# Decoder layer on one core: low parts of q, k and the row maxima by a negative identity in PSUM and ScalarE copies, and three more halves by C on VectorE

## What is computed

```python
# mixer, state scan in chunks of 64 tokens, 512 channels x 16 states
delta = softplus(dlt @ W_dt.T + b_dt)
dA, dBu = exp(delta x A), delta * Bm * u
carry = dA * carry + dBu;  y = sum_n carry[.., n] * C[.., n]
x = layernorm(x + (y * silu(res)) @ W_out.T + b_out)
# cross-attention
q, k, v = x @ w_q.T + b_q, ctx @ w_k.T + b_k, ctx @ w_v.T + b_v
x = layernorm(x + softmax(q k^T / sqrt(16)) v @ w_o.T + b_o)
# experts
x = layernorm(x + (silu(x @ w1) * (x @ w3)) @ w2)
```

## Time and profile before

| | |
|---|---|
| three runs | 2802.23, 2810.59, 2811.07 us, median 2810.59 |
| span of the profiled execution | 2799.9 us (the page gives no other time for it) |
| PE busy | 2426.5 us, 87% |
| DVE busy | 2139.4 us, 76% |
| ACT busy | 1804.7 us, 64% |
| POOL busy | 2075.6 us, 74% |
| granted TensorE clock, mean | 0.955 |

### The profile page before, as it was taken

The page is one execution under the profiler, slowest core; times in us unless marked ns, Lnnn a source line. Parts: engine busy times, 40 slices in busy tenths (PEclk is TensorE's granted clock), DMA queues, the critical chain, the costliest instruction groups (busy, mean ns, idle before and its releaser), DMA issues. The chain is left out here.

```text
span 2799.9 us, 49777 instructions
## 1 busy us (share of the span) xinstructions
PE 2426.5 (87%) x14816; PEld 1658.8 (59%) x14816; DVE 2139.4 (76%) x3586; ACT 1804.7 (64%) x3972; POOL 2075.6 (74%) x968
## 2 busy tenths in 40 slices
PE   3678888888888888988888889988887869999998
PEld 2355666666666666666666666666665545555554
DVE  1778999999999999999999999999999622322332
ACT  1666878878888888788777878778887531211111
POOL 2999999999999999999999999999999300000000
PEclk8788999999999999999999999999998869999999
DMA  3455676656666666666666666665666350243221
GB/s 117 128 133 149 154 168 166 157 157 157 165 167 161 157 167 174 160 171 170 163 166 162 164 165 171 169 169 159 157 166 158 92 159 12 86 128 98 78 78 31
DMA packets 319323, 399.65 MB, mean 143 GB/s; under 512 B 115697, under 2 KB 256241, under 8 KB 314962
## 3 DMA queue, kind: packets, MB, share of 16 engines
q1 hardware_dynamic: 303698, 384.91, 52.9%
q10 hardware_dynamic: 15360, 11.55, 1.5%
HBM read 300.86 MB, written 94.37 MB: 141 GB/s over the span
## 5 line engine op out<-in xcount | busy, mean ns | idle before, releaser
L496 POOL TENSOR_TENSOR arena<-arena 128x1024 f32<-128x1024 f32 x512 | 1209.3, 2366 | 59.6 <-DMA arena<-w_dram 35.4
L572 ACT ACTIVATE dA_ps<-arena,a_neg 128x252 f32<-128x252 f32 x2048 | 868.9, 461 | 327.7 <-DVE dA_ps L777 171.8
L754 DVE TENSOR_TENSOR_SCAN arena<-dA_ps,arena 128x512 f32<-128x512 f32 x672 | 803.4, 1208 | 110.6 <-ACT dA_ps L572 92.2
L506 POOL TENSOR_TENSOR arena<-arena 128x1024 f32<-128x1024 f32 (+1 forms) x416 | 809.1, 1945 | 16.3 <-DVE arena L754 15.3
L754 DVE TENSOR_TENSOR_SCAN dA_ps<-dA_ps,arena 128x512 f32<-128x512 f32 x352 | 416.3, 1206 | 4.8 <-POOL arena L496 3.7
L819 DVE TENSOR_REDUCE mx<-s_ps 128x2 f32<-128x512 f32 x512 | 344.3, 672 | 35.5 <-PE s_ps L877 35.5
L877 PE MATMUL a_ps<-xT,w_conv 128*128 128x256 f32 x1536 | 368.0, 389 | 0.0
L630 ACT ACTIVATE probs<-st_ps 128x512 f32<-128x512 f32 x512 | 296.6, 579 | 42.0 <-PE st_ps L877 34.9
L877 PEld LDWEIGHTS a_ps<-xT,w_conv 128*128 128x128 f32 x1536 | 287.2, 193 | 53.7 <-issue 16.5
L877 PE MATMUL s_ps<-k_st,q_st 96*128 96x256 f32 x1024 | 269.6, 346 | 48.6 <-DVE mx L819 35.1
L877 PE MATMUL y_ps<-arena,sel 128*32 128x256 f32 x4096 | 259.4, 395 | 52.7 <-DVE m_rows L825 28.5
(11 more groups left out here) (105 smaller groups left out, 3213.4 us busy)
## 6 DMA issues: line engine op xcount, KB each, us to landing
arena<-delta_dram SPq DMA_DIRECT2D x512, 128.0 KB, 2.9
arena<-w_dram SPq DMA_DIRECT2D x512, 128.0 KB, 3.3
arena<-bc_dram SPq DMA_DIRECT2D x128, 256.0 KB, 4.5
q_st<-q_parts_dram SPq DMA_DIRECT2D x512, 64.0 KB
k_st<-k_parts_dram SPq DMA_DIRECT2D x512, 64.0 KB
w_dram<-u SPq DMA_DIRECT2D x32, 512.0 KB, 3.1
delta_dram<-delta SPq DMA_DIRECT2D x32, 512.0 KB, 3.9
k_parts_dram<-parts SPq DMA_DIRECT2D x32, 512.0 KB, 3.9
```

The lines of the kernel that those rows point to most:

```text
L496: pool.tensor_tensor(dBu[:, n % NB], w_r[:, n // RP % 2, t % RP].unsqueeze(1).to_broadcast([P, QS, L]), bc_r[:, b.par, 0], ALU.mult).then_ ...
L506: pool.tensor_tensor(h[:, n % NH, states], h[:, n % NH, states], bc_r[:, b.par, 1, states], ALU.mult).then_inc(s_hC, 1)
L572: last = nc.scalar.activation(dA[n % NDA][:, q, :, 1:], delta_r[:, n // (2 * RP) % 2, t % RP].rearrange("p (c t) -> p c t", t=CH)[:, :, 1: ...
L754: nc.vector.tensor_tensor_scan(dst, decays, dBu[:, n % NB, 2 * half:2 * half + 2].rearrange("p q t -> p (q t)"), 0.0, ALU.mult, ALU.add).t ...
```

## The change

`low` for q and k and `max_low` become two steps each. TensorE adds a negative identity times the high part to the value that still stands in PSUM (`less_high`, one matmul of 128x512 into `a_ps`; `max_less_high`, one of 8x128 into `y_ps`), and ScalarE copies what is left (`low`, `max_low`, now in ScalarE's block). The maxima now keep their sign, and the constant rows of `k_st` are -1 in place of 1. `x1T_evac` moves from VectorE, slot 9, to ScalarE, slot 8. `HC_DVE` gets (3, 1), (12, 1) and (13, 1), so VectorE multiplies 14 halves, and GpSimd's product of tiles 3, 12 and 13 shrinks from 1024 to 512 columns.

```diff
-HC_DVE = [(1, 0), (1, 1), (4, 1), (5, 0), (5, 1), (6, 1), (8, 0), (9, 1), (10, 0), (10, 1), (14, 1)]
+HC_DVE = [(1, 0), (1, 1), (3, 1), (4, 1), (5, 0), (5, 1), (6, 1), (8, 0), (9, 1), (10, 0), (10, 1), (12, 1), (13, 1), (14, 1)]
...
-            nc.gpsimd.memset(k_st[4 * DK:4 * DK + 2].bitcast(F32), 1.0).then_inc(s_const_p, 1)
+            nc.gpsimd.memset(k_st[4 * DK:4 * DK + 2].bitcast(F32), -1.0).then_inc(s_const_p, 1)
...
+            def low(s_rest, s_lo):
+                def piece(b):
+                    act.wait_ge(s_rest, b.value(1, 1))
+                    nc.scalar.activation(parts[:, 1], a_ps[:], ACT.Copy).then_inc(s_lo, 1)
...
-                    nc.scalar.activation(m_rows[:, gr % 2, 0], y_ps[0:HG * TT, L:], ACT.Copy,
-                                         scale=-1.0).then_inc(s_m_hi, 1)
+                    nc.scalar.activation(m_rows[:, gr % 2, 0], y_ps[0:HG * TT, L:], ACT.Copy).then_inc(s_m_hi, 1)
...
+            def max_low(gr):
+                def piece(b):
+                    act.wait_ge(s_m_rest, b.value(NG, gr + 1))
+                    nc.scalar.activation(m_rows[:, gr % 2, 1], y_ps[0:HG * TT, L:], ACT.Copy).then_inc(s_m_lo, 1)
...
+                (O_K + 1, low(s_k_rest, s_k_lo)),
+                (O_Q + 1, low(s_q_rest, s_q_lo)),
                 *[(O_SCAN + t - 1, decay(t, 1)) for t in range(NU)],
+                *[(O_MT + HG * gr + 1, max_low(gr)) for gr in range(NG)],
                 *[(O_E + hd, softmax_exp(hd)) for hd in range(H)],
+                (O_X1T, x1T_evac),
...
+            nc.vector.tensor_scalar(neg_id[:], ident[:], -1.0, None, ALU.mult).then_inc(s_neg, 1)
...
-            def low(s_hi, s_lo):
-                    nc.vector.tensor_tensor(parts[:, 1], a_ps[:], parts[:, 0].bitcast(F32),
-                                            ALU.subtract).then_inc(s_lo, 1)
...
-                    nc.vector.scalar_tensor_tensor(out=m_rows[:, gr % 2, 1], in0=y_ps[0:HG * TT, L:], scalar=-1.0,
-                                                   in1=m_rows[:, gr % 2, 0].bitcast(F32), op0=ALU.mult,
-                                                   op1=ALU.subtract).then_inc(s_m_lo, 1)
...
+            def less_high(s_hi, s_rest):
+                    pe.wait_ge(s_hi, b.value(1, 1))
+                    nc.tensor.matmul(a_ps[:], neg_id[:], parts[:, 0], start=False, stop=True,
+                                     skip_group_check=True).then_inc(s_rest, 1)
+            def max_less_high(gr):
+                    pe.wait_ge(s_m_hi, b.value(NG, gr + 1))
+                    nc.tensor.matmul(y_ps[0:HG * TT, L:], neg_id[0:HG * TT, 0:HG * TT], m_rows[:, gr % 2, 0],
+                                     start=False, stop=True, skip_group_check=True).then_inc(s_m_rest, 1)
...
+                (O_K + 1, less_high(s_k_hi, s_k_rest)),
+                (O_Q + 1, less_high(s_q_hi, s_q_rest)),
...
                 *[(O_S + hd, scores(hd)) for hd in range(H)],
+                *[(O_MT + HG * gr + 1, max_less_high(gr)) for gr in range(NG)],
                 *[(O_SCAN + 4 * m + 4, state_sum(m)) for m in range(ND)],
```

More of the change, by code:

```diff
@@ L213, in mixers @@
         ident = shared.ident
+        neg_id = sb("neg_id", [P, P], F32R)
         sel = sb("sel", [P, CT])
@@ L272, in mixers @@
         s_const_a = sem("const_set_act")
+        s_neg = sem("neg_id_set")
         s_xT, s_ctxT, s_xtok = sem("xT_loaded"), sem("ctxT_loaded"), sem("x_tok_loaded")
@@ L291, in mixers @@
         s_x1T_mm, s_x1T = sem("x1T_transposed"), sem("x1T_ready")
[L292 to L293 removed]
+        s_q_mm, s_q_hi, s_q_rest, s_q_lo = sem("q_done"), sem("q_high"), sem("q_less_high"), sem("q_low")
+        s_k_mm, s_k_hi, s_k_rest, s_k_lo = sem("k_done"), sem("k_high"), sem("k_less_high"), sem("k_low")
         s_v_mm, s_v = sem("v_done"), sem("v_ready")
@@ L297, in mixers @@
         s_s_mm, s_max = sem("scores_done"), sem("max_done")
-        s_mT_mm, s_m_hi, s_m_lo = sem("max_transposed"), sem("max_high"), sem("max_low")
+        s_mT_mm, s_m_hi, s_m_rest, s_m_lo = sem("max_transposed"), sem("max_high"), sem("max_less_high"), sem("max_low")
         s_m_dram, s_m_row = sem("max_in_dram"), sem("max_rows_loaded")
@@ L610, in high, with x1T_evac @@
                 return piece
+            def low(s_rest, s_lo):
+                def piece(b):
+                    act.wait_ge(s_rest, b.value(1, 1))
+                    nc.scalar.activation(parts[:, 1], a_ps[:], ACT.Copy).then_inc(s_lo, 1)
+                return piece
+            def x1T_evac(b):
+                act.wait_ge(s_x1T_mm, b.value(1, 1))
+                if b.back(3):
+                    act.wait_ge(s_of_mm, b.back(3).value(TT, TT))
+                nc.scalar.activation(x1T[:], a_ps[:], ACT.Copy).then_inc(s_x1T, 1)
             def bc_store(b):
@@ L847, in head_norm @@
                 return piece
[L849 to L853, removed]
             run_steps([
@@ L866, in _ @@
                 *[(O_SCAN + t, clear_starts(t, half)) for t, half in HC_DVE],
-                (O_Q + 1, low(s_q_hi, s_q_lo)),
-                *[(O_MT + HG * gr + 1, max_low(gr)) for gr in range(NG)],
             ], B)
@@ L1010, in q_proj, with piece @@
                 return piece
+            def less_high(s_hi, s_rest):
+                def piece(b):
+                    if not b.back(1):
+                        pe.wait_ge(s_neg, 1)
+                    pe.wait_ge(s_hi, b.value(1, 1))
+                    nc.tensor.matmul(a_ps[:], neg_id[:], parts[:, 0], start=False, stop=True,
+                                     skip_group_check=True).then_inc(s_rest, 1)
+                return piece
+            def max_less_high(gr):
+                def piece(b):
+                    pe.wait_ge(s_m_hi, b.value(NG, gr + 1))
+                    nc.tensor.matmul(y_ps[0:HG * TT, L:], neg_id[0:HG * TT, 0:HG * TT], m_rows[:, gr % 2, 0],
+                                     start=False, stop=True, skip_group_check=True).then_inc(s_m_rest, 1)
+                return piece
             def scores(hd):
```

5 lines of the change are left out of this document (removed).

## The result

The changed kernel takes 2997.35 us (median of 4 runs, 2983.97 to 3007.95), the kernel before 2810.83 us in the same comparison: ratio 1.067, 95% interval 1.063 to 1.070. It is slower by 187 us. The forecast was slower by 110 us, 2920 us, with a range of 2780 to 2970: the sign was right, the size too small, and the time lies above the range, next to the rival in which ScalarE falls out of step (2980 us).

A forecast was written before the change was run, and what follows sets the result against it. A loop over TensorE, VectorE and ScalarE was taken as the bound, not GpSimd. Terms 0.6 + 0 + 1.2 + 0.7 + 0.85 + 0.3 = 3.7 us a batch, times 30, gave 110 us: 2920 us, range 2780 to 2970.

The forecast's parts named there:

- the rival in which ScalarE falls out of step: ScalarE, held at six places for TensorE, delivers scan exponentials late and VectorE stands too: 2980 us, chance 12%.
- a loop over TensorE, VectorE and ScalarE: Claimed bound: the chain changes between these three engines, GpSimd keeps up beside it; only work on the chain counts.
- The rival by which the most contended engine is to be relieved first: GpSimd, the busiest engine, is the bound and its 3.27 us a batch come off: 2715 us, chance 14%.
- slot 5: ScalarE's new copy waits for TensorE's matmul, with softmax exponential and first layer norm behind it: +0.7 us a batch.
- ScalarE held behind the copies of slots 13 and 1: Same mechanism as for the maxima in slot 5, with less behind it: +0.3 us a batch, bounds 0 to 0.7.
- The trips: TensorE idles while ScalarE copies a matmul's result: 0.7 or 0.6 us per maxima trip, 1.2 us each for q and k.
- q and k: Low parts in slots 12 and 0: q +0.6 us a batch, k 0 because its trip fits an existing TensorE wait.
- VectorE's relief: VectorE's net -0.9 us a batch, but +0.5 us from 1051 to 1066 beside a later TensorE: costs nothing, saves nothing.
- ScalarE's stretch: Slots 8 to 10, where ScalarE is the chain: x1T copy and one low part add 0.85 us a batch.
- The hidden trips: Rival: TensorE's idle time is mostly slack and takes up its waits for ScalarE's copies: 2780 to 2811 us, chance 16%.
- the sign of the forecast: Expected: L487 spacing 70 us, four `y_ps<-arena,sel` waits a batch of 0.4 us or more, GpSimd under 90%.

The follow-up runs named there:

- e_hc14: The kernel before with only VectorE's 14 halves added, taken over from GpSimd: 2848.2 us, ratio 1.015.
- e_hold_15: The kernel before, with ScalarE waiting for TensorE's scores in slots 1 and 5 only, copying nothing: 2940.1 us, ratio 1.048.
- e_busy: The kernel before with six more TensorE matmuls (0.72 us) ahead of each of the four state sums, nothing held on ScalarE: 2845.5 us, ratio 1.013.
- e_hold: The kernel before, with ScalarE waiting for TensorE's scores at the four places of the low-maxima copies, copying nothing: 2938.6 us, ratio 1.047.
- e_max_undone: The changed kernel with the maxima made as before; q, k, x1T and the 14 halves stay changed: 2859.8 us, ratio 1.018 to the kernel before.
- e_early: The changed kernel with all four matmuls of the maxima moved ahead on TensorE, right behind `pv`: 3016.9 us, ratio 1.073 to the kernel before.
- e_oT_first: The changed kernel with ScalarE's evacuation of oT moved ahead, right behind the copy of the low maxima: 2960.3 us, ratio 1.055 to the kernel before.

## Why the prediction went wrong, point by point

**The bound.** Right that GpSimd is not it: in e_hc14, GpSimd's 3.3 us a batch less bought nothing. That the bound is a loop over TensorE, VectorE and ScalarE fits the runs (time added on TensorE, on VectorE or on ScalarE each made the kernel slower, and each by less than was added), but no run isolates the loop. The rival by which the most contended engine is to be relieved first (the Trainium skill, Perfetto Trace Analysis, Identifying the Most-Contended Engine) would have had 2715 us; the runs of this kernel do not bear it out, since here GpSimd had 97% of the window and almost no one waited for it.

**The step that failed: ScalarE's hold in slots 5 and 1.** The sum had 0.7 us for slot 5, and 0.3 us for "ScalarE held behind the copies of slots 13 and 1". Measured, the waits of slots 1 and 5 alone cost 130 us (e_hold_15), 4.3 us a batch at 30 batches, and those of slots 9 and 13 4 us. Of the 5.2 us by which a batch grew in the profiled execution of e_hold_15 (its slowest), 2.4 are idle time of TensorE, still over twice the 1.0 of the sum, and the rest is its lower clock, which the changed kernel does not have. The mechanism was in the text, even the norm behind the copy, but I followed it only to the next softmax exponential and priced slot 1 as having less behind it. It has as much: the second layer norm. And I left out the bank `f_ps`: the gate projection waits for oT, 2.5 us a batch in the changed kernel (71.5 us / 28). The trace of before shows no wait for oT at all, so no row asked for a price; the order showed that oT stands behind the norm. The bound on these terms, 0.7 and 1.2 us, was too narrow for the same reason. The range had a slip of its own: the bounds as listed add up to 1.5 and 6.7 us, not 1.7 and 5.8, and the measured 5.7 us lies inside them; the cut to 5 us left it out. The right sign is no proof of the sum: two of its gaps, the hold and the halves, both made it too small.

**The trips.** Sized right as TensorE's time, and counted too fully. The new matmul takes 0.22 us against 0.2, the waits ahead of the state sums are 0.5 us, the one for q 0.8: the pieces are as forecast. But e_busy shows that TensorE's added time reaches the end only to some 40%. What the four trips of the maxima cost beside the hold stays open, since e_hold and e_max_undone differ in clock.

**q and k.** 0.6 us a batch, measured 34 us alone, 1.1 us at 30 batches: size half. TensorE's waits for the trips fitted into its idle time, for q more fully than I had it; what shows is about the work of the two new matmuls, 1 us. Taken off the whole change they show nothing.

**VectorE's relief and the halves.** "It costs nothing, and saves nothing" was wrong by 39 us for the halves alone, 1.3 us a batch at 30 batches. I had set them against a TensorE that would be late anyway. With three matmuls early they cost 25 us; inside the change as it stands they were not taken back alone.

**x1T.** Forecast 0.59 us of 0.85 on ScalarE's stretch, measured 11 us, some 0.35 us a batch: 0.6 of the size. The mechanism shows: the wait ahead of slot 9's state sum, once a batch, grew from 1.0 to 1.5 us, which is 14 us over 28 batches.

**Rivals.** ScalarE out of step had 12% and 2980 us, and comes nearest to what happened, in slots 1 and 5 and not, as its text had it, in 13 and 1. The hidden trips did not show. What was named as the sign of the forecast did show: a spacing of 70 us (72.3), waits ahead of `y_ps<-arena,sel` four times a batch, GpSimd at 85% of the window.

**The parts do not add.** Hold 130, halves 39, q and k 34, x1T 11 us, and 36 us for TensorE's time make 250 us, and the change costs 187. A part taken off the whole (q and k: 2 us) and the same part put on the base (34 us) differ. Two causes are possible, and were not separated: the larger wait hides the smaller, and the clock is another one in each kernel. If the hold is counted by its idle time alone, it is 2.6 us a batch, some 80 us (an estimate from the table). What of the 187 us falls to the maxima's matmuls, copies and trips beside the hold was not isolated and stays open.

## What to carry to other kernels

Before a wait is put into an engine's fixed order, list what stands behind it until the engine would have been idle anyway, and follow each of these pieces to its reader: here the price was set by readers without slack, and TensorE's wait for oT was one that no row of before shows. An engine that often stands idle may have a lead over another, as ScalarE had here, and the lead is used up by a wait for that other engine put in front of long work; the same wait behind the long work cost a quarter (34 us in place of 132). To price a part, run it on the base as well as taken off the whole. And compare the idle and the busy time of TensorE apart: in e_early and e_oT_first its idle time fell as the theory said, and a lower granted clock took all or most of it back.

## What the runs showed of the hardware

The granted clock of TensorE fell after waits. In e_early, once a batch TensorE is idle for 3.88 us; the windows around it (columns as in the earlier trace rows):

```profile
1045.00:1050.00 5.00, 1.81 (x21) 1.02 (x21) 3.74 (x6) 4.94 (x6) 5.00 (x3) 1.00 1.04 176
1050.00:1055.00 5.00, 4.01 (x15) 2.67 (x19) 3.29 (x4) 3.77 (x11) 4.17 (x3) 0.68 0.14 17
...
1060.00:1065.00 5.00, 3.63 (x16) 2.65 (x16) 2.50 (x7) 4.97 (x11) 4.33 (x2) 1.00 0.58 168
1065.00:1070.00 5.00, 4.22 (x13) 2.92 (x13) 2.30 (x3) 1.39 (x4) 4.67 (x3) 0.66 0.36 131
```

TensorE is busy 1.81 of 5 us, and in the next 5 us the mean granted clock is 0.68: for more than half of the stretch the lower level, 1.2 GHz, was granted. Fifteen microseconds later the same happens after a stretch with 3.63 us busy. Over 500 to 2000 us e_early has a mean clock of 0.92, where the changed kernel has 1.00. TensorE's busy time is 64.2 us a batch against 60.0 with the same matmuls, and its idle time 9.7 against 12.3: what e_early lost on the changed kernel is a slower TensorE, and not more waiting. Not every wait was followed by the lower level. In the changed kernel's timeline the gate projection stood for 1.32 us and then took 2.00 us; in e_hold_15 it stood for 1.69 us and then took 3.68.
